# A two-layer graph kernel: the first edge stage sums into a transposed accumulator

## The chip, the cores and the metric

One core of a Trainium2 chip. The metric is the device time of one execution in microseconds (us), the median of three runs. The engines are TensorE (PE; its weight loads PEld), VectorE (DVE), ScalarE (ACT), GpSimd (POOL) and SyncE (SP), with 16 DMA engines beside them. TensorE's clock has two levels, 1.2 and 2.4 GHz; the profile gives the granted clock as a share of the higher one.

## The reference, cut to what matters

6250 nodes with 256 features, 100000 edges sorted by destination, 64 attributes for each edge. First layer:

```
h   = relu(layernorm(x))
e   = relu(edge_attr @ ee_w1 + ee_b1) @ ee_w2 + ee_b2
agg = segment_sum(h[src] + e, dst)      # each node also has an edge to itself, with attributes 0
t   = (1 + eps) * h + agg
t   = relu(ln(t @ w1 + b1)); t = relu(ln(t @ w2 + b2)); y = t @ w3 + b3
x   = x + relu(ln(h + y))
```

The second layer is graph attention over the same edges: scores from both end nodes, a softmax over the edges of a destination, a weighted sum of features, added to x. The change does not touch it.

Since `@ ee_w2` is linear, the kernel sums `relu(edge_attr @ ee_w1 + ee_b1)`, here r, over a node's edges and multiplies the sum by ee_w2 afterwards, once for each node.

## The kernel before, in words

Nodes lie in 50 tiles of 125. An accumulator `acc` [128, 50, 512] in float32 stays in SBUF: for each node (a partition) 256 sums of node features and 256 sums of r. There are five blocks with a barrier after each, and in a block each engine runs its own list of instructions, written out by hand and tied by semaphores.

**Preparation** (`prepare`). Ten chunks c of five tiles. VectorE takes the statistics (`stats`, L264 and L267), ScalarE the root (`deviation`, L216), VectorE the coefficients (L272, L273), ScalarE normalises in place (L222), GpSimd adds ee_b2 into `ht` (L201). ScalarE's `high` (L229) and VectorE's `low` (L284) split `ht` into two float16 halves in `tb`, two slots, which SyncE stores as the gather table `tab0` (L182). VectorE's `own` (L280) writes (2 + eps) times the normalised row plus ee_b2 back into the first half of `acc`. The second half of `acc` starts at zero: half the tiles by GpSimd (L195), half by ScalarE (L232). ScalarE's order is `high(c-2)`, `deviation(c)`, the normalisation of c; VectorE's is `low(c-2)`, `own(c-1)`, `stats(c+1)`, `coefficients(c+1)`. Last on ScalarE is a small DMA of a row of the edge weights (L242), issued after its last `high`, for which it waits; SyncE waits for all stores of the table.

**First edge stage** (`edges0`). 196 batches of 512 edges. GpSimd issues four indirect gathers for each batch (L446) into a ring of six. TensorE computes the edge layer (`edge_mlp`, 8 float16 matmuls of 256 columns, L500 and L501), ScalarE and VectorE split the result into halves (L478, L579). VectorE builds a one-hot matrix edge by node (L325). `sums` then multiplies it with the gathered rows and with r, high and low halves: for each 128 edges the one-hot is the stationary operand and 256 features are the moving one, four matmuls (L507 to L510), 16 for a batch. Where a batch reaches a further tile, `sums` runs once more; it runs 245 times in all. VectorE adds the PSUM tile [125, 512] to the accumulator at a tile index that is read at run time (L556, L569).

**Dense stage** (`nodes`). A software pipeline over tiles: step i does the first layer of tile i, the second layer of tile i-1, the output of tile i-2, and later parts of i-3 and i-4; steps 4 to 47 run in a loop of two. Here features lie on partitions and nodes on the free axis, so the accumulator has to be turned: GpSimd copies tile i+2 of it to `ur` (L813), TensorE's `turn` transposes the r half with two transposes (L868), ScalarE adds the self edge's relu(ee_b1) in `turned` (L1024). `make_h` multiplies by ee_w2 with four float32 matmuls (L918, L922) and turns and adds the own part with two more against the identity (L919), in PSUM. ScalarE's `high_h` (L1070) and VectorE's `low_h` (L1200) split h into halves; `low_h` releases the first layer (semaphore h_split). A float32 matmul is two records in the trace.

TensorE's order in a step i: wait h_split, `layer1(i)`, in it `variance(1)`; two transposes for the scores (L977); wait a_split[0]; `layer2(i-1)`, first half and a quarter of the second, then `variance(0)` for tile i, then the rest; score products; wait a_split[1]; three of eight parts of `output(i-2)`; `make_h(i+1)`; `turn(i+2)`; the rest of the output. layer1 has 48 matmuls, layer2 192, all of 125 columns, the output 24 of 256.

ScalarE's order in a step: `turned`, bias of layer 1 (L1031), deviation(1), bias, squares (L1051), the scores' h2h, `activated(1)` and `high(1)`, deviation(0), bias of layer 2 in two halves (L1031), then `activated(0)`, eight activations (L1059) with `high_h` between the fourth and the fifth, and `high(0)` (L1065). VectorE's `low(0)` (L1189), early in the next step, releases a_split[0]. Late in a step VectorE has scaled(0), row_norm(1), squares (L1165), the score row, `low_h`. GpSimd folds squares (L829 to L831), and clears the accumulator for the second layer (L840) when `make_h` has released it.

The second edge stage and the finish follow; they have the same shape of code before and after.

Of the kernel before, what the change touches and what calls it, by code (L numbers as in the profile page):

```python
# [32 lines left out]
P = 128  # L33
N, D, E, ED, H = 6250, 256, 100000, 64, 1024
TN = 125
# [76 lines left out]
def prepare(nc, t, dram, sb):  # L112


    with ExitStack() as ctx:
        m = Memory(nc, ctx)
        acc, rstd, nmr = sb["acc"], sb["rstd0"], sb["nmr0"]
        CH = NT // PG
# [8 lines left out]
        b2bc = m.sb("p_b2bc", [TN, D], F32)  # L127
        eps1 = m.sb("eps1", [P, 1], F32)
        er = m.sb("er", [P, D], F32)
# [12 lines left out]
        spans_sb = m.sb("spans_sb", [half, 2, 2], I32)  # L142

# [7 lines left out]
        tb_ready, t_free = m.sem("tb_ready"), m.sem("t_free")  # L151
        tb_stored = [m.sem(f"tb_stored{s}") for s in range(2)]
# [35 lines left out]
        def _(pool):  # L188
# [6 lines left out]
            pool.memset(acc[:, 0:NT // 2, D:2 * D], 0.0)  # L195
# [10 lines left out]
        def _(act):  # L206
            act.dma_start(b2bc[:], t["L0_gnn_ee_b2"].partition_broadcast(TN)).then_inc(ld_small, 16)
# [22 lines left out]

            act.wait_ge(consts, 1)
            act.activation(acc[:, NT // 2:NT, D:2 * D], sb["lneps"][:].unsqueeze(2).broadcast_to([P, NT - NT // 2, D]), ACT.Copy, scale=0.0)  # L232
# [10 lines left out]
            act.wait_ge(ewb_done, 16)  # L243

        @block.vector
        def _(dve):
# [29 lines left out]
            def own(c):  # L276

                h = acc[0:TN, tiles(c), 0:D]
                dve.wait_ge(t_ready, c + 1)
                settled(dve.scalar_tensor_tensor(out=h, in0=h, scalar=eps1[0:TN, :], in1=ht[:, c % 2], op0=ALU.mult, op1=ALU.add))  # L280
# [11 lines left out]
            dve.wait_ge(ld_small, 16 * 6)  # L292
            settled(dve.tensor_scalar(eps1[:], eps1[:], 1.0, None, ALU.add))
            settled(dve.tensor_copy(sb["ewa"][:], er[:]))
# [12 lines left out]
            for c in range(CH + 2):  # L307
                if c >= 2:
                    low(c - 2)
                if 1 <= c < CH:  # L310
                    own(c - 1)
# [3 lines left out]
            own(CH - 1)  # L315
# [27 lines left out]
def edges0(nc, t, dram, sb):  # L343


    with ExitStack() as ctx:
# [23 lines left out]
        sum_ps = m.ps("sum_ps", [TN, 3, 2 * D])  # L370
# [120 lines left out]
        def _(pe):  # L491
# [1423 lines left out]
```

## Time and profile before

| | us |
|---|---|
| median of 3 runs | 3159.29 (3156.21 to 3159.81) |
| span of the profiled execution | 3157.3 |
| preparation, to the first instruction of the edge stage | 93.0 |
| first gather issued | 94.1 |
| start of the dense stage | 1107.8 |

Over the whole span TensorE is busy 2446.9 us (77%), VectorE 2156.6 (68%), GpSimd 1976.9 (63%), ScalarE 1488.6 (47%), and the mean granted clock is 0.906. The profiled execution's own time is not listed apart from its span; the span lies 2.0 us under the median of the runs. Busy time is the time in which an engine has an instruction in it; matmuls overlap each other, so neighbouring starts, not durations, tell TensorE's speed. An idle time in brackets names what ended it, "PEq L982" for example the engine's own wait at that line.

### The profile page before, as it was taken

Reading aid. Unit: us, or ns where it says so; the run is one execution under the profiler, and the core shown is the slowest. Engines: PE = TensorE matmul, PEld = TensorE weight load, DVE = VectorE, ACT = ScalarE, POOL = GpSimd, SP = SyncE. Lnnn points to the kernel's source line nnn. Section 1 sums busy time; section 2 is a strip of 40 time slices with the busy share of each in tenths; the row PEclk is TensorE's granted clock in tenths of the full one; section 3 lists DMA queues with packets and bytes.
Section 4 is the critical chain, followed back from the end, with each engine's and each line's share of the span. In section 5 each row is a group of like instructions: output and inputs, shape, how many; then the busy total and the mean of one; then the engine's idle time right before and its main releaser. Section 6 shows DMA issues by size and latency. Waiting matters only on the chain. (4 is left out here: it accounts for less than half of the span.)

```text
span 3157.3 us, 79016 instructions
## 1 busy us (share of the span) xinstructions
PE 2446.9 (77%) x25310; PEld 2164.9 (69%) x25311; DVE 2156.6 (68%) x3833; ACT 1488.6 (47%) x3803; POOL 1976.9 (63%) x2143
## 2 busy tenths in 40 slices
PE   0577777777777789999999999947777777777763
PEld 0466666666666679999999999945555555555552
DVE  7676667777677636666666666657766766666666
ACT  5444444444444458888888888831111111111114
POOL 4677777777777634444444444437777777777772
PEclk9998889999899889999999999978888888887996
DMA  6555555555555500000000000026555655555554
GB/s 158 168 161 149 158 154 166 161 163 160 159 164 158 143 25 18 21 21 20 20 21 20 20 22 21 21 61 178 171 173 173 174 172 168 173 172 173 171 170 136
DMA packets 183839, 373.69 MB, mean 118 GB/s; under 512 B 42598, under 2 KB 93688, under 8 KB 183769
## 3 DMA queue, kind: packets, MB, share of 16 engines
q0 software_dynamic: 75552, 209.66, 23.5%
q1 hardware_dynamic: 107392, 162.37, 17.4%
q10 hardware_dynamic: 824, 0.87, 0.1%
q8 instruction: 27, 0.44, 0.1%
q14 instruction: 44, 0.35, 0.0%
HBM read 346.95 MB, written 25.80 MB: 118 GB/s over the span
## 5 line engine op out<-in xcount | busy, mean ns | idle before, releaser
L446 POOL DMA_INDIRECT rows<-tab_scratch,srcs x784 | 765.7, 977 | 238.7 <-issue 234.1
L1458 POOL DMA_INDIRECT a_rows<-tab_scratch,srcs x784 | 750.5, 957 | 251.7 <-issue 235.8
L1524 PE MATMUL sum_ps<-feat,a_hot 128*125 128x264 f32 x1960 | 601.5, 463 | 237.5 <-DVE feat L1616 121.0
L1524 PEld LDWEIGHTS sum_ps<-feat,a_hot 128*125 128x125 f32 x1960 | 417.4, 222 | 341.7 <-DVE feat L1616 133.9
L876 PE MATMUL z_ps<-ah,w 128*128 128x125 f16 x6400 | 553.8, 219 | 1.0 <-PEq L982 1.0
L876 PE MATMUL z_ps<-al,w 128*128 128x125 f16 x3200 | 542.7, 217 | 0.0
L876 PEld LDWEIGHTS z_ps<-ah,w 128*128 128x128 f16 x6400 | 489.5, 97 | 1.5 <-issue 1.4
L1468 ACT ACTIVATE feat<-d 128x32 f32<-128x32 f32 x196 | 44.9, 229 | 827.0 <-DVE d L1612 566.2
L500 PE MATMUL mlp_ps<-ewa,eab 128*128 128x256 f16 x788 | 203.5, 290 | 284.3 <-PEq L496 283.3
L478 ACT ACTIVATE rh<-mlp_ps 128x1024 f16<-128x1024 f32 x196 | 199.7, 1019 | 358.2 <-ACTq L477 347.7
L829 POOL TENSOR_TENSOR a<-a 128x500 f32<-128x500 f32 x100 | 124.4, 1244 | 372.1 <-POOLq L828 372.1
L507 PE MATMUL sum_ps<-rows,hot 128*125 128x256 f16 x980 | 296.4, 302 | 76.8 <-DMA rows<-tab_scratch,srcs 55.8
L1059 ACT ACTIVATE a<-z,pack 128x125 f32<-128x125 f32 x800 | 321.4, 484 | 11.9 <-ACTq L1055 7.8
L876 PEld LDWEIGHTS z_ps<-al,w 128*128 128x128 f16 x3200 | 315.2, 98 | 0.8
L500 PEld LDWEIGHTS mlp_ps<-ewa,eab 128*128 128x128 f16 x788 | 81.9, 104 | 327.4 <-issue 315.1
L509 PE MATMUL sum_ps<-rh,hot 128*125 128x256 f16 x980 | 291.2, 297 | 0.0
L508 PE MATMUL sum_ps<-rows,hot 128*125 128x256 f16 x980 | 291.1, 297 | 0.0
L510 PE MATMUL sum_ps<-rl,hot 128*125 128x256 f16 x980 | 289.9, 296 | 0.0
L579 DVE SCALAR_TENSOR_TENSOR rl<-mlp_ps,rh 128x1024 f16<-128x1024 f32 x196 | 240.0, 1225 | 34.3 <-DVEq L578 29.2
L1031 ACT ACTIVATE z<-z_ps,pack 128x125 f32<-128x125 f32 x800 | 226.3, 371 | 37.5 <-ACTq L1029 37.5
L1616 DVE TENSOR_TENSOR feat<-a_rows,p_ps 128x1024 f32<-128x1024 f32 x196 | 239.1, 1220 | 3.9 <-DVEq L1404 0.5
L507 PEld LDWEIGHTS sum_ps<-rows,hot 128*125 128x125 f16 x980 | 148.3, 151 | 116.9 <-DMA rows<-tab_scratch,srcs 71.0
(211 smaller groups left out, 5422.8 us busy)
## 6 DMA issues: line engine op xcount, KB each, us to landing
ea<-edge_t SPq DMA_DIRECT2D x394, 128.0 KB
dstb<-dst_flat SPq DMA_DIRECT2D x98, 512.0 KB
rows<-tab_scratch,srcs POOLq DMA_INDIRECT x784
a_rows<-tab_scratch,srcs POOLq DMA_INDIRECT x784
tab_scratch<-prow SPq DMA_DIRECT2D x50, 128.9 KB
hx<-x SPq DMA_DIRECT2D x50, 125.0 KB
x_scratch<-x SPq DMA_DIRECT2D x50, 125.0 KB
hs<-tab_scratch SPq DMA_DIRECT2D x50, 125.0 KB
```

Source lines behind the costliest of these rows:

```text
L446: pool.indirect_dma_start(rows[:, b % DEEP, k, :], None, dram["tab0"], bass.IndirectOffsetOnAxis(ap=srcs[:, c:c + 1], axis=0),).then_inc(r ...
L500: pe.matmul(mlp_ps[:, s, k, :], eab[:, s, e], ewa[:], start=True, stop=False)
L507: pe.matmul(out[:, 0:D], lhs, rows[:, ring, k, 0:D], start=(k == 0), stop=False, skip_group_check=True)
L508: pe.matmul(out[:, 0:D], lhs, rows[:, ring, k, D:2 * D], start=False, stop=False, skip_group_check=True)
L509: pe.matmul(out[:, D:2 * D], lhs, rh[:, s, k, :], start=False, stop=False, skip_group_check=True)
L510: ins = pe.matmul(out[:, D:2 * D], lhs, rl[:, s, k, :], start=False, stop=(k == CB - 1), skip_group_check=True)
L579: dve.scalar_tensor_tensor(out=rl[:, s].rearrange("p k d -> p (k d)"), in0=mlp_ps[:, s].rearrange("p k d -> p (k d)"), scalar=0.0, in1=rh[ ...
L876: ins = pe.matmul(out, lhs, rhs, start=(k == 0 and q == 0), stop=(k == n - 1 and q == 2))
L1059: ins = act.activation(a[j][:, k, :], z[j][:, k, :], ACT.Relu, bias=cols[be][:, k:k + 1], scale=cols[g][:, k:k + 1])
L1458: pool.indirect_dma_start(rows[:, b % DEEP, k, :], None, dram["tab1"], bass.IndirectOffsetOnAxis(ap=srcs[:, c:c + 1], axis=0),).then_inc(r ...
L1524: ins = pe.matmul(out[:], hot[:, h, k, :], feat[:, row, k, :], start=(k == 0), stop=(k == CB - 1))
L1616: return dve.tensor_tensor(feat[:, u, :, 0:D].rearrange("p k (h f) -> p k h f", h=HEADS), slot_of(slot)[:, :, 0:D].rearrange("p k (h f) -> ...
```

## The change

The accumulator of the first layer is kept turned: `accT` is the same memory seen as [128 features, tile, q, 128 nodes], q = 0, 1 for the two halves of the node features and q = 2, 3 for those of r. In `sums` the gathered rows and r become the stationary operand, 128 features wide, and the one-hot the moving one, 125 columns: 32 matmuls for a batch rather than 16. VectorE adds [128, 4, 125]. In the preparation TensorE turns each chunk of the table (20 float16 matmuls against an identity, high and low halves), and ScalarE and VectorE each write one half of the features, scaled and shifted, into `accT`; the self edge's relu(ee_b1) is the start value of the r half. ScalarE's `own(c-3)` stands ahead of `high(c-2)`, and the small DMA of the edge weights' row stands behind the last `own`. In the dense stage GpSimd's copy, `turn`, `turned` and the two own matmuls of `make_h` are gone; `make_h(i+1)` reads `accT` directly and stands behind `variance(0)`, inside the second layer; a new instruction `whole_h` on VectorE adds its PSUM result and the own part into `h32` in SBUF, and `high_h` and `low_h` read that. Variances share a bank and wait for each other's reader (v_read).

```diff
@@ prepare, ScalarE
+            def own(c):
+                act.wait_ge(own_done, c + 1)
+                act.activation(accT[:, tiles(c), 0, 0:TN], own_ps[c % 2][0][:, 0:PG, 0:TN], ACT.Identity,
+                               bias=own_off[:, 0:1], scale=eps2[:]).then_inc(own_kept[0], 1)
...
-            for c in range(CH + 2):
-                if c >= 2:
+            act.wait_ge(own_coef, 1)
+            for c in range(CH + 3):
+                if c >= 3:
+                    own(c - 3)
+                if 2 <= c < CH + 2:
                     high(c - 2)
@@ prepare, TensorE (new)
+            for c in range(CH):
+                pe.wait_ge(tb_ready, c + 1)
+                if c >= 2:
+                    for j in range(KD):
+                        pe.wait_ge(own_kept[j], c - 1)
+                for k in range(PG):
+                    for j in range(KD):
+                        out = own_ps[c % 2][j][:, k, 0:TN]
+                        pe.matmul(out, tb[:, c % 2, k, j * P:(j + 1) * P], ident16[0:TN, 0:TN], start=True, stop=False)
+                        ins = pe.matmul(out, tb[:, c % 2, k, D + j * P:D + (j + 1) * P], ident16[0:TN, 0:TN], start=False, stop=True)
+                ins.then_inc(own_done, 1)
@@ prepare, VectorE
-                dve.wait_ge(t_ready, c + 1)
-                settled(dve.scalar_tensor_tensor(out=h, in0=h, scalar=eps1[0:TN, :], in1=ht[:, c % 2], op0=ALU.mult, op1=ALU.add))
+                dve.wait_ge(own_done, c + 1)
+                dve.tensor_scalar(accT[:, tiles(c), 1, 0:TN], own_ps[c % 2][1][:, 0:PG, 0:TN], eps2[:], own_off[:, 1:2],
+                                  ALU.mult, ALU.add).then_inc(own_kept[1], 1)
@@ edges0, sums
-                    lhs = hot[:, h, k, :]
-                    pe.matmul(out[:, 0:D], lhs, rows[:, ring, k, 0:D], start=(k == 0), stop=False, skip_group_check=True)
...
+                    rhs = hot[:, h, k, :]
+                    for q in range(2 * KD):
...
+                        to = out[:, q, 0:TN]
+                        pe.matmul(to, high, rhs, start=(k == 0 and q == 0), stop=False, skip_group_check=True)
+                        ins = pe.matmul(to, low, rhs, start=False, stop=(k == CB - 1), skip_group_check=True)
@@ nodes, TensorE
-            def make_h(i, p):
...
+            def make_h(i):
                 for j in range(KD):
-                    f = slice(j * P, (j + 1) * P)
-                    pe.matmul(h_ps[:, j, :], w2e[:, 0, f], rt[:, 0, :], start=True, stop=False)
-                    own = pe.matmul(h_ps[:, j, :], ur[:, p, f], ident[0:TN, 0:TN], start=False, stop=False)
...
+                    for k in range(KD):
+                        r = accT[:, bass.ds(i, 1), KD + k, 0:TN].rearrange("p a n -> p (a n)")
+                        ins = pe.matmul(h_ps[:, j, :], w2e[:, k, j * P:(j + 1) * P], r, start=(k == 0), stop=(k == KD - 1))
                 ins.then_inc(h_done, 1)
...
                 if has(i, 0):
                     variance(0)
+                if has(i, 0, 1):
+                    make_h(i + 1)
                 if has(i, 1):
                     layer2(1, range(1, 4), 1 - p)
...
-                    output(range(FIRST))
-                if has(i, 0, 1):
-                    make_h(i + 1, 1 - p)
-                if has(i, 0, 2):
-                    turn(i + 2, p)
-                if has(i, 2):
-                    output(range(FIRST, KH)).then_inc(y_done, 1)
+                    output(range(KH)).then_inc(y_done, 1)
@@ nodes, ScalarE
-                if has(i, 0, 1):
-                    turned(i + 1)
@@ nodes, VectorE
+            def whole_h(i):
+                dve.wait_ge(h_done, 1)
+                dve.sem_inc(h_done, -1)
+                a_own = accT[:, bass.ds(i, 1), 0:KD, 0:TN].rearrange("p a q n -> p (a q) n")
+                dve.tensor_tensor(h32[:], h_ps[:], a_own, ALU.add).then_inc(h_ready, 1)
...
                     row_norm(1, h2[:], x1[:]).then_inc(h2_ready, 1)
+                if has(i, 0, 1):
+                    whole_h(i + 1)
                 if has(i, 1):
                     squares()
```

## Rows read from the trace of the kernel before

**Rows 1.** Stretches (us, busy and instructions of each engine, TensorE's granted clock, DMA share, GB/s).

```profile
93.00:1107.00 1014.00, 743.89 (x5496) 646.62 (x5496) 718.42 (x923) 443.60 (x614) 766.65 (x785) 0.90 0.55 159
1300.00:2000.00 700.00, 700.00 (x10679) 698.61 (x10678) 468.22 (x772) 600.90 (x1619) 307.62 (x407) 1.00 0.07 20
```

**Rows 2.** Groups by shape, first edge stage, 150 to 1100 us (busy, mean ns | idle before, releasers).

```profile
L446 POOL DMA_INDIRECT rows<-tab_scratch,srcs x741 | 723.5, 976 | 225.7 <-issue 221.2 <-DVEq L560 4.6
...
L478 ACT ACTIVATE rh<-mlp_ps 128x1024 f16<-128x1024 f32 x185 | 188.5, 1019 | 344.0 <-ACTq L477 333.4 <-ACTq L475 7.9 <-issue 2.2
...
L507 PEld LDWEIGHTS sum_ps<-rows,hot 128*125 128x125 f16 x928 | 140.4, 151 | 107.5 <-DMA rows<-tab_scratch,srcs 68.4 <-issue 36.9
```

**Rows 3.** Groups by shape, dense stage, 1300 to 2000 us.

```profile
L876 PEld LDWEIGHTS z_ps<-ah,w 128*128 128x128 f16 x4719 | 360.4, 97 | 0.0
```

**Rows 4.** Timeline of a regular dense tile (start us, us, instruction [idle before <-releaser]).

```profile
1601.61 0.28 PE L876 MATMUL gp_ps<-waug,h2h 128*125 128x272 f16 x1
...
1603.29 0.38 PE L918 MATMUL hv_ps<-rt,w2e 128*128 128x125 f32 x2
...
1604.63 0.38 PE L868 MATMUL tv_ps<-ident,ur 125*128 125x125 f32 x2
1604.84 0.27 PE L876 MATMUL y_ps<-w,ah 128*125 128x256 f16 x1
1604.91 0.38 ACT L1070 ACTIVATE hh<-hv_ps 128x250 f16<-128x250 f32 x1 [0.38 <-ACTq L1069]
...
1608.12 1.20 DVE L1189 TENSOR_TENSOR al<-a,ah 128x1000 f16<-128x1000 f32 x1 [0.78 <-DVEq L1188]
...
1609.64 0.22 PE L876 MATMUL z_ps<-ah,w 128*128 128x125 f16 x1
...
1620.65 0.28 PE L876 MATMUL gp_ps<-waug,h2h 128*125 128x272 f16 x1
```

**Rows 5.** The low part of h: duration min/median/max, first and last start.

```profile
L1200 DVE SCALAR_TENSOR_TENSOR hl<-hv_ps,hh x50: 418/419/420, 1115.6 to 2043.4; 128x250 f16<-128x250 f32 x50
```

**Rows 6.** Timeline of tile 1 of the dense stage.

```profile
1134.43 0.21 PE L876 MATMUL z_ps<-ah,w 128*128 128x125 f16 x1 [0.34 <-PEq L982]
...
1145.42 0.44 PE L918 MATMUL hv_ps<-rt,w2e 128*128 128x125 f32 x2
...
1146.98 1.20 DVE L1165 TENSOR_TENSOR a<-z 128x1000 f32<-128x1000 f32 x1 [2.40 <-DVEq L1164]
...
1148.24 0.38 ACT L1070 ACTIVATE hh<-hv_ps 128x250 f16<-128x250 f32 x1
...
1148.76 0.42 DVE L1200 SCALAR_TENSOR_TENSOR hl<-hv_ps,hh 128x250 f16<-128x250 f32 x1 [0.58 <-DVEq L1199]
...
1149.32 0.21 PE L876 MATMUL z_ps<-hh,w 128*128 128x125 f16 x1 [2.13 <-PEq L958]
...
1151.44 1.20 DVE L1189 TENSOR_TENSOR al<-a,ah 128x1000 f16<-128x1000 f32 x1 [2.26 <-DVEq L1188]
```

**Rows 7.** Timeline of the preparation and the start of the edge stage.

```profile
43.93 1.27 ACT L229 ACTIVATE tb<-ht 125x1280 f16<-125x1280 f32 x1 [4.80 <-DMA tab_scratch<-tb]
...
78.26 0.30 ACT L216 ACTIVATE rstd<-mv,lneps 125x5 f32<-125x5 f32 x1 [2.04 <-DVE mv L267]
...
79.01 1.49 DVE L284 TENSOR_TENSOR tb<-ht,tb 125x1280 f16<-125x1280 f32 x1
...
80.84 1.55 DVE L280 SCALAR_TENSOR_TENSOR acc<-acc,eps,ht 125x1280 f32<-125x1280 f32 x1 [0.34 <-DVEq L250]
...
85.25 0.59 ACTq L242 DMA_DIRECT2D ewb<-ebh  x1
86.82 1.49 DVE L284 TENSOR_TENSOR tb<-ht,tb 125x1280 f16<-125x1280 f32 x1 [0.34 <-DVEq L250]
...
93.03 0.69 SPq L406 DMA_DIRECT2D st<-sched_scratch  x1
...
95.85 0.73 DVE L325 SCALAR_TENSOR_TENSOR hot<-dsts,negbase,e_iota_ps 128x500 f16<-128x500 f32 x1 [2.39 <-DMA st<-sched_scratch]
```

More of the change, by code:

```diff
@@ L142, in prepare @@
         spans_sb = m.sb("spans_sb", [half, 2, 2], I32)
+        own_ps = [[m.ps(f"own{s}{j}_ps", [P, 8, P]) for j in range(KD)] for s in range(2)]
         ld_x = [m.sem(f"ld_x{c}") for c in range(CH)]
@@ L151, in prepare @@
         tb_ready, t_free = m.sem("tb_ready"), m.sem("t_free")
+        ld_ecol, own_coef, own_done = m.sem("ld_ecol"), m.sem("own_coef"), m.sem("own_done")
+        own_kept = [m.sem(f"own_kept{j}") for j in range(KD)]
         tb_stored = [m.sem(f"tb_stored{s}") for s in range(2)]
@@ L305, in _ @@
             dve.tensor_copy(spans_sb[:], sched_sb[:].rearrange("p c j -> p j c")).then_inc(sched_ready, 1)
-            for c in range(CH + 2):
-                if c >= 2:
+            for c in range(CH + 3):
+                if 2 <= c < CH + 2:
                     low(c - 2)
-                if 1 <= c < CH:
-                    own(c - 1)
+                if c >= 3:
+                    own(c - 3)
                 if c + 1 < CH:
@@ L314, in _ @@
                     coefficients(c + 1)
-            own(CH - 1)
+            for j in range(KD):
+                dve.wait_ge(own_kept[j], CH)
     return range(m.sems[0].num, m.sems[-1].num + 1)
@@ L732, in nodes @@
         hx_free, h0_ready = sem("hx_free"), sem("h0_ready")
-        v1_read = sem("v1_read")
-        ur_ready, ur_free = sem("ur_ready"), sem("ur_free")
-        t_done, rt_ready = sem("t_done"), sem("rt_ready")
-        h_done, hh_ready, h_split = sem("h_done"), sem("hh_ready"), sem("h_split")
+        v_read = sem("v_read")
+        acc_free = sem("acc_free")
+        h_done, h_ready, hh_ready, h_split = sem("h_done"), sem("h_ready"), sem("hh_ready"), sem("h_split")
         z_done = [sem(f"z{j}_done") for j in (1, 2)]
@@ L862, in _ @@
         def _(pe):
-            def turn(i, p):
-                pe.wait_ge(ur_ready, 1)
-                pe.sem_inc(ur_ready, -1)
-                for k in range(KD):
-                    ins = pe.transpose(t_ps[:, k, :], ur[:, p, D + k * P:D + (k + 1) * P], ident[0:TN, 0:TN])
-                ins.then_inc(t_done, 1)
             def products(out, hi, lo, whi, wlo, n, ks=None, rows=False):
@@ L942, in scores @@
                 ins.then_inc(att_done, 1)
-            turn(0, 0)
             bias_sums()
             pe.wait_ge(ld_w2e, 16)
-            pe.wait_ge(rt_ready, 1)
-            pe.sem_inc(rt_ready, -1)
-            make_h(0, 0)
-            turn(1, 1)
+            make_h(0)
             def body(i, p):
@@ L1017, in _ @@
             act.dma_start(bpack[:, 0:4 * D], t["rows_pack"].partition_broadcast(TN)).then_inc(ld_rows, 16)
-            act.wait_ge(eb_ready, 1)
-            def turned(i):
-                act.wait_ge(t_done, 1)
-                act.sem_inc(t_done, -1)
-                for k in range(KD):
-                    ins = act.activation(rt[:, k, :], t_ps[:, k, :], ACT.Identity, bias=eb1[:, k:k + 1])
-                ins.then_inc(rt_ready, 1)
             def biased(j, b, half):
@@ L1172, in chain_done, with inverse @@
                 dve.sem_inc(chain_sem, -1)
-            def inverse(j, read=None):
+            def inverse(j):
                 dve.wait_ge(sd_ready[j], 1)
                 dve.sem_inc(sd_ready[j], -1)
-                if read is not None:
-                    dve.sem_inc(read, 1)
+                dve.sem_inc(v_read, 1)
                 dve.reciprocal(rstd[j][:], rstd[j][:]).then_inc(rstd_ready, 1)
@@ L1199, in low_h @@
                 dve.sem_inc(hh_ready, -1)
[L1200 removed]
+                dve.scalar_tensor_tensor(out=hl[:], in0=h32[:], scalar=1.0 / WS, in1=hh[:],
                                          op0=ALU.mult, op1=ALU.subtract).then_inc(h_split, 1)
+            def whole_h(i):
[3 more added lines that the diff above has]
+                dve.tensor_tensor(h32[:], h_ps[:], a_own, ALU.add).then_inc(h_ready, 1)
+            whole_h(0)
             low_h()
+            dve.sem_inc(acc_free, 1)
             score_parts()
@@ L1272, in body @@
                     low_h()
+                    dve.sem_inc(acc_free, 1)
                 if has(i, 4):
```

99 lines of the change are left out of this document (51 added, 48 removed).

## The prediction

> **What bounds the kernel now.** I read the stretches first [rows 1]. There are two stages that the change touches for long. In the first edge stage (93 to 1107 us) TensorE is busy for 744 of 1014 us at a mean granted clock of 0.90; in the dense stage (about 1108 to 2108 us, here its regular part) it is busy for 700.00 of 700 us at 1.00. The busy time of a pipelined engine alone is no proof, so the groups come next. In the edge stage GpSimd's gathers take 723.5 us of a stretch of 950, and the idle time before them is 225.7 us, of which 221.2 is its own issue and 4.6 a wait [rows 2]: 949.2 of 950, so GpSimd's gathers set the pace, 5.1 us for each batch of four, and TensorE, VectorE and ScalarE have slack. In the dense stage TensorE streams without a pause, one tile in 19.04 us: (2043.4 - 1148.76) / 47 = 19.03 [rows 5, 6]. But the second limit is close behind, and this is what the whole forecast hangs on.
>
> **The loop behind TensorE.** Call Z the end of a tile's second layer and X the start of the next tile's. TensorE does from Z (1601.61) to X (1609.64) score products, output, make_h with the turns, and the next first layer: 8.03 us [rows 4]. From X to the next Z (1620.65) it needs 11.01 us. Beside this runs a chain: Z, then ScalarE's second half of the bias, four activations, the high part of h, four activations, the high part of the activations, and VectorE's low part of them, which releases X. That low part starts at 1608.12 and takes 1.20, so it ends at 1609.32 [rows 4]; TensorE arrives 0.32 us after that, of which the release takes about 0.15. Slack is under 0.2 us. In that chain ScalarE waits 0.38 us for make_h, until 1604.91 [rows 4]. How long the chain is without that wait is shown by tile 1, where TensorE has no output to compute and make_h comes right behind Z: Z at 1145.42, the high part of h at 1148.24 with no idle before it, the low part at 1151.44 to 1152.64. That is 7.22 us; the same tile's X came at 1134.43 after a wait of 0.34 [rows 6], and X to Z was 10.99. TensorE is released 0.14 us after a VectorE instruction ends (1148.76 + 0.42 to 1149.32) [rows 6]. So the chain Z to X is 7.22 + 0.15 = 7.37 us, and a tile that is bound by it takes 10.99 + 7.37 = 18.36.
>
> **Dense stage, part by part.** Removed from TensorE: two transposes, 1604.84 - 1604.63 = 0.21 us, and two of six float32 matmuls, which take (1604.63 - 1603.29) / 6 = 0.223 each, so 0.45 [rows 4]: 0.66 us a tile, 33 us over 50 tiles if TensorE stayed the bound. But the four matmuls that remain, 0.89 us, are also moved: from between Z and X, where all 1.55 us of make_h and turn stood, to behind variance(0), between X and Z. TensorE's own work from Z to X falls to 8.03 - 1.55 = 6.48 us, less than the chain's 7.37, so the chain decides there. From X to Z it rises to 11.01 + 0.89 = 11.90. New period: 11.90 + 7.37 = 19.27 against 19.04, a loss of 0.23 us a tile. TensorE will wait 0.9 us a tile, in two places: for h_split before the first layer (in tile 1 the low part of h ends at Z + 3.76 [rows 6]; TensorE is ready at Z + 1.68 for the score products and nine output matmuls [rows 4], + 1.64 for fifteen more at 0.11, = 3.32), with the release about 0.6 us, and 0.3 for a_split[0] before the second. Nothing is on the wait's back: behind it in TensorE's queue are just these layers.
> Other edits of the stage: whole_h on VectorE is 250 elements of PSUM and SBUF, priced as the low part of h, 0.42 us [rows 5]. It stands between the row normalisation and the squares, which wait for the bias until Z + 1.56 (1146.98 in tile 1 [rows 6]), so the idle time there hides it; were it not hidden, it would delay the squares of tile i-1, whose variance is wanted 5 us later. ScalarE's two turned activations and GpSimd's copy go; both engines are idle for longer than that and neither piece is in the chain (turned comes after the high part). The wait of v_read is met by the reciprocal issued microseconds before. acc_free stands in front of GpSimd's clearing and its folding, and it is given 3 us before the folding has input. Reading h from SBUF rather than PSUM: from 0 to 0.03 us. Registers for the address of acc on TensorE: hidden by its backlog, up to 0.1 us a tile if not.
> Sum: tiles 1 to 3 lack output or score products and stand nearer to the chain's 18.36; to 19.27 they lose up to 0.9 each, 2.7 us. The other 45 lose 0.23 each, 10.4 us. The start loses a turn, its activations and its hops, at half clock: I take -1.2. The end 0. Together +11.9; bounds: the wait could be 0.1 us a tile shorter or 0.2 longer, +7 to +21.
>
> **First edge stage.** 16 matmuls of 256 columns become 32 of 125 for each batch. Weights were 125 wide and loaded in 151 ns [rows 2]; they become 128 wide, as in the dense stage, where a load takes 97 ns and hides [rows 3]: (11.01 - 0.28) / 192 = 0.056 us for each 125-column matmul at full clock. 32 of them take 1.79 us; 16 of 256 columns at 0.11 (1.68 us for six of 272 and nine of 256 [rows 4]) took 1.76. Cost 0 us of 5.1 us a batch, and TensorE's slack covers more than that. VectorE's add has 500 elements for 512. Value 0, bounds -3 to +6, since the gathers' time (976 ns in the mean [rows 2]) varies with what VectorE does.
> A rule speaks against this part. The Trainium skill (TensorE: Matmul & The Clock Gate, section The mechanism) says that a weight load overlaps running matmuls only if its row group differs. All loads here use all rows, so by it load and stream would take turns. The rows deny it: the 97 ns load fits beside a step of 56 ns. What it would cost is a rival below.
>
> **Preparation.** Each chunk of 5 tiles now also goes through TensorE: 20 matmuls of 125 columns. The engine is otherwise idle here, so I take half clock, 0.11 us each: 2.2 us, and 0.4 for start and drain. VectorE loses 1.55 us [rows 7] and gains an instruction over 625 elements. ScalarE gains 0.7, between 0.38 (250 elements) and 1.02 (1024) [rows 2, 4]. VectorE's own, 625 elements, is taken at 0.8 between its 0.42 for 250 and 1.49 for 1280 [rows 5, 7]. The order matters more: ScalarE's own(c-3) stands ahead of high(c-2), the square root of the next statistics and all that follows. Today ScalarE idles 2.04 us before that square root [rows 7]. From the start of VectorE's split (79.01): 1.49 split, 0.25 semaphores, 2.4 TensorE, 0.15, own 0.7, high 1.2, root 0.3, coefficients 0.4 with their hops: 6.75, against 6.63 now. So 0.1 us a chunk, on six chunks behind the wait of 4.80 us for the stores at 43.93 [rows 7], which swallows what the later start (one more DMA in ScalarE's queue, three small VectorE instructions) costs before it. The end is where it shows: high(9) comes after own(8), which waits for TensorE on the split of chunk 8. That split starts at 79.6 + 6.1 and ends 7.6 later than 79.6; TensorE 2.5, own 0.7, high 1.2, the last split 1.5: it ends at 93.2, not 88.31 [rows 7]. Then own(9) (2.5 + 0.8), and only then the small DMA of the bias row, which was issued at 85.25 before; from issue to use such a DMA took 2.8 us (93.03 to 95.85) [rows 7]. The stage ends at 99.7 instead of 93.03: +6.7, bounds +2 (if the order costs only at the last chunk) to +10.
>
> **Sum** against the profiled execution (span 3157.3 us, which is 2.0 below the median of 3159.3, the runs before spread from 3156.2 to 3159.8): 6.7 + 0 + 11.9 = +18.6, so 3178 us on the scale of the runs. The later stages are not touched.
>
> **Rivals.**
> A, faster: TensorE stays the bound of the dense stage. It needs the chain from Z to X to be shorter than 6.48 us; tile 1 measured 7.22 plus release, and the steady tile 7.71 with a wait of 0.38 and hops. Then the period is 19.04 - 0.66 = 18.38, 50 tiles give -33, with +6.7 for the preparation: 3133 us. For it speaks 700.00 of 700 busy; against it the row of tile 1. Chance 0.13.
> B, as forecast but the preparation is free, since VectorE has 0.7 us less a chunk: 3171 us. Against it the order on ScalarE. Chance 0.10.
> C, load and stream in turn (the rule above): 97 + 56 = 153 ns a matmul, by 32 in 245 groups (196 batches and 49 extra tiles) is 1200 us; the edge MLP's 1568 at 0.11 add 172; 1372 us against the gathers' 784 by 949.2 / 741 = 1004: +368, and 3178 with it is 3546 us. Chance 0.01.
> D, the waits in the dense stage bring the clock down. The edge stage has 0.90 at 73% busy, the dense one 1.00 at 100% [rows 1]. At 0.90 in the dense stage the 11.9 us from X to Z become 13.2: +1.3 by 48, 3240 us. But the waits are 0.9 of 19.3 us, in two pieces. Chance 0.04.
> E, the same mechanism with smaller numbers in both places (a chain 0.15 shorter, the preparation +2): 3164 us. Chance 0.10.
> The forecast itself, 3168 to 3190: 0.62.
>
> **Chances.** A measurement of this kernel tells 0.2% (6.3 us) from no change. Faster: A with some of E's tail, 0.14. Same (3153 to 3165.6): the most of E and a little of B, 0.12. Slower: 0.74. The range, 3158 to 3191, leaves out A, C and D, and about as little of the forecast on either side.
>
> **What would show it.** Right: dense period about 19.27, ScalarE's high part of h without idle before it, TensorE waiting at the h_split and a_split[0] lines, X to Z 11.9; gathers still back to back in the edge stage, its length within 5 us; the first gather at about 101 us instead of 94. Wrong: a period of 18.4 with TensorE full (A), the first gather at 94 (B), TensorE's step over 0.1 us at full clock (C), granted clock under 0.97 in the dense stage (D).

## The result, and the profile after

After the change the kernel takes 3205.24 us in the median (3203.65 to 3206.87, four runs); the kernel before, run beside it on the same chip, takes 3159.55 (3156.21 to 3160.64). The ratio is 1.0144, 95% interval 1.013 to 1.0159: slower by 45.7 us. The forecast was 3178 us with a range of 3158 to 3191: the direction was right, the size was not, and the time lies outside the range.

The two profiled executions (spans 3157.3 and 3204.5) differ by stage as follows. Each stage ends with the first instruction of the next one; "the rest" is the second edge stage and the finish.

| us | before | after | difference | forecast |
|---|---|---|---|---|
| preparation | 93.0 | 105.7 | +12.7 | +6.7 |
| first edge stage | 1014.8 | 1015.9 | +1.1 | 0 |
| dense stage | 1006.1 | 1040.4 | +34.3 | +11.9 |
| the rest | 1043.4 | 1042.6 | -0.8 | 0 |

Stretches of the kernel after, as [rows 1]: the edge stage from its start over the same length, and the regular part of the dense stage.

```profile
106.00:1120.00 1014.00, 748.51 (x9416) 661.73 (x9416) 715.65 (x922) 445.15 (x614) 762.90 (x785) 0.89 0.55 159
1300.00:2000.00 700.00, 659.62 (x10101) 651.01 (x10099) 504.20 (x786) 568.64 (x1498) 276.15 (x355) 1.00 0.07 20
```

The edge stage is as it was, though TensorE issues 9416 instructions for 5496. In the dense stage TensorE now has holes, 40.4 us in 700, at a granted clock that is still 1.00. VectorE is busy 36 us more. The new whole_h explains 36 x 0.41 = 15 of them; the other 21 call for an explanation. The waits of TensorE in the same 700 us put all 40.4 at one line, the wait for h_split (us in total, times, longest):

```profile
PE z_ps L909 <- PEq L982: 40.4, 36, 1.1
```

The groups by shape of the kernel after, edge stage (150 to 1100 us) and dense stage, answer to [rows 2] and [rows 3]:

```profile
L491 POOL DMA_INDIRECT rows<-tab_scratch,srcs x742 | 720.9, 972 | 230.6 <-issue 221.1 <-DVEq L610 9.4
...
L560 PEld LDWEIGHTS sum_ps<-hot,rows 128*128 128x128 f16 x1870 | 198.2, 106 | 2.4
...
L909 PEld LDWEIGHTS z_ps<-ah,w 128*128 128x128 f16 x4531 | 346.4, 97 | 0.0
```

Gathers still stand back to back: 720.9 us in them and 221.1 of their own issue in the 950 us, and 9.4 of waiting. A 128-column weight load takes 106 ns in the edge stage, where the mean granted clock is 0.89, and the stage is no longer for having twice as many of them.

Why the h_split wait is long is in the timelines of one regular tile, VectorE first, then GpSimd, then TensorE, which answer to [rows 4]:

```profile
1618.05 0.43 DVE L1282 SCALAR_TENSOR_TENSOR prow<-gp_ps,bpack 125x272 f32<-125x272 f32 x1
1618.74 1.08 DVE L1202 SCALAR_TENSOR_TENSOR hl<-h,hh 128x250 f16<-128x250 f32 x1 [0.26 <-DVEq L1201]
1619.75 0.64 DVE L1290 COPY st<-prow 125x16 f32 x1
```

```profile
1618.31 1.24 POOL L872 TENSOR_TENSOR a<-a 128x500 f32<-128x500 f32 x1 [4.06 <-POOLq L871]
1619.73 0.63 POOL L873 TENSOR_TENSOR a<-a 128x250 f32<-128x250 f32 x1 [0.18 <-POOLq L866]
```

```profile
1619.97 0.21 PE L909 MATMUL z_ps<-hh,w 128*128 128x125 f16 x1 [1.12 <-PEq L982]
```

The low part of h is 250 elements on 128 partitions, 0.42 us before [rows 5]. Here it takes 1.08: it starts inside GpSimd's fold (1618.31 to 1619.55) and ends 0.27 us after it. TensorE starts the first layer 0.15 us later, after 1.12 us of waiting where 0.6 was forecast. All 50 low parts of h (ns, min/median/max):

```profile
L1202 DVE SCALAR_TENSOR_TENSOR hl<-h,hh x50: 420/1082/1483, 1128.7 to 2090.5; 128x250 f16<-128x250 f32 x50
```

Its operand has moved: h was in PSUM before (`hv_ps`) and is in SBUF now (`h`, in the code `h32`). SBUF as such isn't slow, since the minimum is 0.42. In 48 of the 50 tiles GpSimd's fold had begun before it, and in each of them it ends 0.27 or 0.28 us after the fold. Tile 2 shows the same pair, VectorE and then GpSimd:

```profile
1165.17 1.08 DVE L1202 SCALAR_TENSOR_TENSOR hl<-h,hh 128x250 f16<-128x250 f32 x1 [0.61 <-DVEq L1201]
```

```profile
1164.74 1.24 POOL L872 TENSOR_TENSOR a<-a 128x500 f32<-128x500 f32 x1 [9.37 <-POOLq L871]
```

GpSimd ends at 1165.98, VectorE at 1166.25: again 0.27 later. The two others took 0.42. For tile 0 GpSimd had nothing running (its next instruction began at 1129.88); for tile 1 a copy on GpSimd began 0.21 us after it:

```profile
1128.70 0.42 DVE L1202 SCALAR_TENSOR_TENSOR hl<-h,hh 128x250 f16<-128x250 f32 x1 [0.69 <-DVEq L1201]
...
1145.00 0.42 DVE L1202 SCALAR_TENSOR_TENSOR hl<-h,hh 128x250 f16<-128x250 f32 x1 [1.88 <-DVEq L1201]
1145.21 0.47 POOL L880 COPY acc<-zero 125x264 f32<-125x264 f32 x1 [6.49 <-POOLq L879]
```

An instruction with one tensor input can be held too. The copy `st<-prow` behind the low part of h takes 0.64 us inside GpSimd's second fold (the row of 1619.75 above), and 0.17 in the kernel before, where it starts 0.10 us ahead of that fold (at 1605.87 and 1605.97).

The start of the preparation shows the same thing larger. VectorE and GpSimd of the kernel after:

```profile
15.24 0.15 DVE L332 TENSOR_SCALAR eps<-eps 128x1 f32<-128x1 f32 x1 [6.07 <-DMA eps<-L_gnn_eps]
15.55 7.36 DVE L333 TENSOR_SCALAR own_off<-ecol,eps 128x2 f32<-128x2 f32 x1
...
24.75 1.41 DVE L302 BATCH_NORM_STATS2 stat<-acc 125x6 f32<-125x256 f32 x4 [0.24 <-DVEq L288]
```

```profile
6.32 16.56 POOL L205 TENSOR_SCALAR acc<-ecol 128x3200 f32<-128x3200 f32 x2 [4.04 <-DMA ecol<-cols_pack]
```

An instruction over two elements takes 7.36 us: GpSimd's two new fills (8.28 us each, relu(ee_b1) into its half of `accT`) run until 22.88, and VectorE's instruction ends at 22.91. The first statistics start at 24.75, against 15.46 in the kernel before.

### The profile page after: what moved, and what is told of

Same layout as the page of the kernel before. It is cut to its first block and busy times, and to the rows that moved or that the text cites. A ratio compares the mean times of both kernels' runs of the same rounds, so it can differ in the third digit from the quotient of the medians.

```text
span 3204.5 us, 86737 instructions
## 1 busy us (share of the span) xinstructions
PE 2460.0 (77%) x29130; PEld 2179.0 (68%) x29131; DVE 2212.8 (69%) x3885; ACT 1481.5 (46%) x3714; POOL 1948.8 (61%) x2094
## 5 line engine op out<-in xcount | busy, mean ns | idle before, releaser
L1537 PE MATMUL sum_ps<-feat,a_hot 128*125 128x264 f32 x1960 | 612.6, 470 | 230.4 <-DVE feat L1629 104.7
L1537 PEld LDWEIGHTS sum_ps<-feat,a_hot 128*125 128x125 f32 x1960 | 427.2, 227 | 331.6 <-issue 129.0
L545 PE MATMUL mlp_ps<-ewa,eab 128*128 128x256 f16 x788 | 211.7, 299 | 230.2 <-PEq L541 222.5
L559 PE MATMUL sum_ps<-hot,rows 128*128 128x125 f16 x1960 | 354.4, 234 | 36.5 <-PEq L581 15.7
L559 PE MATMUL sum_ps<-hot,rh 128*128 128x125 f16 x1960 | 353.1, 233 | 0.0
L560 PE MATMUL sum_ps<-hot,rl 128*128 128x125 f16 x1960 | 352.5, 233 | 0.0
L560 PE MATMUL sum_ps<-hot,rows 128*128 128x125 f16 x1960 | 352.3, 233 | 0.0
L1039 ACT ACTIVATE z<-z_ps,pack 128x125 f32<-128x125 f32 x800 | 225.5, 367 | 99.3 <-ACTq L1037 99.3
L559 PEld LDWEIGHTS sum_ps<-hot,rows 128*128 128x128 f16 x1960 | 205.3, 105 | 71.5 <-issue 46.9
```

Source lines behind the costliest of these rows:

```text
L545: pe.matmul(mlp_ps[:, s, k, :], eab[:, s, e], ewa[:], start=True, stop=False)
L559: pe.matmul(to, high, rhs, start=(k == 0 and q == 0), stop=False, skip_group_check=True)
L560: ins = pe.matmul(to, low, rhs, start=False, stop=(k == CB - 1), skip_group_check=True)
L1039: ins = act.activation(z[j][:, k, :], z_ps[j][:, half, (k % 4) * TN:(k % 4 + 1) * TN], ACT.Identity, bias=cols[b][:, k:k + 1], scale=(1.0, ...
L1537: ins = pe.matmul(out[:], hot[:, h, k, :], feat[:, row, k, :], start=(k == 0), stop=(k == CB - 1))
```

## The experiments

All times are medians; ratios are against the kernel before. The profiled executions gave these stages (us; "low h" is the median duration of the low part of h, "period" the time from one regular dense tile to the next).

| kernel | time | ratio (95%) | prep. | edge | dense | period | low h |
|---|---|---|---|---|---|---|---|
| before | 3159.5 | | 93.0 | 1014.8 | 1006.1 | 19.04 | 0.419 |
| after | 3205.2 | 1.0144 (1.013, 1.0159) | 105.7 | 1015.9 | 1040.4 | 19.66 | 1.082 |
| e1 h in PSUM | 3183.9 | 1.0077 (1.006, 1.0094) | 105.4 | 1012.2 | 1020.7 | 19.25 | 0.419 |
| e4 + make_h back | 3175.5 | 1.0054 (1.0037, 1.007) | 105.0 | 1011.3 | 1012.5 | 19.09 | 0.419 |
| e2 fill by VectorE | 3205.9 | 1.015 (1.0133, 1.0167) | 97.9 | 1020.4 | 1040.3 | 19.66 | 1.082 |
| e2b the same, padded | 3197.4 | 1.0123 (1.0106, 1.0141) | 98.4 | 1012.9 | 1040.8 | 19.65 | 1.081 |
| e3 own behind | 3194.6 | 1.0112 (1.0095, 1.0129) | 94.5 | 1015.6 | 1041.2 | 19.66 | 1.082 |
| e5 = e1 + e2b + e3 | 3167.6 | 1.0028 (1.0018, 1.0038) | 89.1 | 1014.1 | 1019.8 | 19.25 | 0.419 |
| e7 = e1 + two ahead | 3146.2 | 0.9962 (0.9947, 0.9976) | 105.2 | 1012.3 | 978.8 | 18.38 | 0.405 |
| e6 = e5 + two ahead | 3125.6 | 0.9893 (0.9875, 0.9912) | 88.8 | 1015.9 | 978.8 | 18.38 | 0.406 |

**e1: h stays in PSUM.** The rivals for the missing 0.39 us of the period are VectorE's operand in SBUF beside GpSimd's fold, and a chain that was sized wrong for another reason (the new whole_h, its wait, the longer X to Z). Only the place of h changes.

```diff
-                dve.tensor_tensor(h32[:], h_ps[:], a_own, ALU.add)
+                dve.tensor_tensor(h_ps[:], h_ps[:], a_own, ALU.add)
-                act.activation(hh[:], h32[:], ACT.Copy, scale=1.0 / WS)
+                act.activation(hh[:], h_ps[:], ACT.Copy, scale=1.0 / WS)
-                dve.scalar_tensor_tensor(out=hl[:], in0=h32[:], ...
+                dve.scalar_tensor_tensor(out=hl[:], in0=h_ps[:], ...
```

> The changed kernel, with h kept in PSUM: whole_h adds the own part onto the PSUM tile in place, and the high and low parts read that tile instead of h32 in SBUF. Theory (port): VectorE's low part of h takes 1.08 us instead of 0.42 because it now has two operands in SBUF and is held up by GpSimd's fold that runs beside it; this delays h_split, the first layer and so the second layer's start by 0.39 us a tile. Then the low part of h goes back to 0.42 us, the dense period falls from 19.66 to about 19.27 (X to Z 11.90, Z to X 7.37), and the time falls by 17 to 20 us, to about 3186. Rival (the order alone): the period of 19.66 comes from where make_h stands; then nothing moves by more than 3 us and the period stays over 19.6.

Measured: 3183.86 us, 21.4 less than after; the dense stage 19.7 less. The low part of h, all 50 of this kernel, and one of them beside the fold that began before it (VectorE, then GpSimd):

```profile
L1201 DVE SCALAR_TENSOR_TENSOR hl<-h_ps,hh x50: 418/419/419, 1124.7 to 2068.0; 128x250 f16<-128x250 f32 x50
```

```profile
1161.88 0.42 DVE L1201 SCALAR_TENSOR_TENSOR hl<-h_ps,hh 128x250 f16<-128x250 f32 x1 [0.58 <-DVEq L1200]
```

```profile
1161.48 1.24 POOL L871 TENSOR_TENSOR a<-a 128x500 f32<-128x500 f32 x1 [9.37 <-POOLq L870]
```

This is the pair of 1165.17 above with 0.40 us between the two starts in place of 0.43, the same fold beside it, and the operand in PSUM: 0.42 for 1.08. So for this instruction neither the fold nor the SBUF operand costs anything alone; the two together do. The period falls to (2068.0 - 1124.7) / 49 = 19.25 in the mean, 19.253 in the regular part; the forecast for the change was 19.27.

**e4: make_h back in its old place,** on top of e1: between the third and the fourth part of the output, with whole_h behind the squares on VectorE (not in the cut below). It asks what it is worth to have moved the 0.89 us of make_h to between X and Z.

```diff
                 if has(i, 0):
                     variance(0)
-                if has(i, 0, 1):
-                    make_h(i + 1)
...
-                    output(range(KH)).then_inc(y_done, 1)
+                    output(range(3))
+                if has(i, 0, 1):
+                    make_h(i + 1)
+                if has(i, 2):
+                    output(range(3, KH)).then_inc(y_done, 1)
```

> As the first of these (h in PSUM), and make_h put back to its old place, between the parts of the output, with whole_h behind the squares. Theory (the chain from Z to X sets the period together with what TensorE does from X to Z): X to Z falls by 0.89 us to 11.0; the high part of h now waits for make_h, about 0.6 us, so Z to X is about 8.0; the period is about 19.0, 0.65 us less than 19.66 and 0.25 less than the first experiment: about 3175 us. Rival (TensorE's sum of work sets the period, wherever make_h stands): the same time as the first experiment.

Measured: 3175.45 us, period 19.09. Counted from the start of the score transposes, the second layer starts (X) at 0.52 and ends (Z) at 11.52, so X to Z is back at 11.00 (11.89 in e1), but Z to X is 8.09, against 7.36: the high part of h starts at Z + 3.54 instead of Z + 2.8, because it must wait for make_h and whole_h, and the chain is longer by that. TensorE still waits 9.4 us in the 700 at h_split. Moving make_h trades 0.89 us between X and Z for 0.73 in the chain; in neither place is the period shorter than the 19.04 of the kernel before.

**e2 and e2b: the fill goes to VectorE,** before it waits for its small loads. The rivals for the preparation's start are that VectorE was held up by GpSimd's fills, and that the added small instructions and the DMA of the load were late by themselves.

```diff
@@ GpSimd
-            for j in range(KD):
-                pool.tensor_scalar(accT[:, 0:NT // 2, KD + j, :], ecol[:, 0, j:j + 1]... , 0.0, None, ALU.max)
+                # e2b only: two instructions over one element keep the list as long
+                pool.tensor_scalar(ptmp[:, j:j + 1], ecol[:, 0, j:j + 1], 0.0, None, ALU.max)
@@ VectorE
+            dve.wait_ge(ld_ecol, 16)
+            for j in range(KD):
+                settled(dve.tensor_scalar(accT[:, 0:NT // 2, KD + j, :], ecol[:, 0, j:j + 1]... , 0.0, None, ALU.max))
             dve.wait_ge(ld_small, 16 * 6)
```

> The changed kernel, with the start value of half of the accumulator written by VectorE, while it waits for its small loads, instead of by GpSimd (two instructions of 3200 elements a partition). Theory (port): GpSimd's two instructions (8.3 us each) hold up a VectorE instruction over two elements for 7.4 us, and all of the preparation starts late. Then the first statistics start at about 17 us instead of 24.8, and the first gather falls from 106.8 to about 101, since some of the gain is lost to the later wait for the stores: 4 to 8 us less in all, about 3199. Rival (the order on ScalarE is all that costs in the preparation): the first gather stays within 2 us of 106.8 and so does the time.

Measured: 3205.9 us, no gain, and yet the preparation is 7.8 us shorter. VectorE's own start in e2:

```profile
9.15 3.94 DVE L328 TENSOR_SCALAR acc<-ecol 128x3200 f32<-128x3200 f32 x2
14.40 0.15 DVE L331 TENSOR_SCALAR eps<-eps 128x1 f32<-128x1 f32 x1 [1.31 <-DMA eps<-L_gnn_eps]
14.71 0.23 DVE L332 TENSOR_SCALAR own_off<-ecol,eps 128x2 f32<-128x2 f32 x1
...
16.90 1.73 DVE L298 BATCH_NORM_STATS2 stat<-acc 125x6 f32<-125x256 f32 x5 [0.24 <-DVEq L284]
```

The two-element instruction takes 0.23 for 7.36, and the fill itself 3.94 for GpSimd's 16.56. Of the 7.8 us the edge stage took back 4.5 (1020.4 for 1015.9), and what follows the dense stage is 1.6 longer in this execution (1044.1 for 1042.6), which was not traced. The gathers of e2 are all a little longer (min/median/max):

```profile
L490 POOL DMA_INDIRECT rows<-tab_scratch,srcs x784: 952/957/1913, 99.0 to 1107.8; - x196
```

After the change they were 940/946/1771. 784 gathers by 0.011 us are 8.6, which the edge stage did not show in full against the kernel after. The theory for e2b was that the longer gather belongs to GpSimd's list of instructions, which is two shorter, and not to the fill.

> As e2_fill_vector, but GpSimd keeps two instructions in the place of the two that went, each over a single element a partition. In e2 the preparation became 7.9 us shorter, as the port theory has it, but the time did not: each of the 784 gathers of the first edge stage took 0.957 us in the median instead of 0.946, which is 8.6 us. Theory (GpSimd's list of instructions): that step of 0.011 us depends on what stands ahead of the gathers in GpSimd's list, not on the fill; with the list as long as before the median is 0.946 again, the first gather at 99, and the time about 3198. Rival (what VectorE's shorter start does to the stage): the median stays at 0.957 and the time at 3205.

Measured: 3197.39 us, 7.9 under after; edge stage 1012.9, and the gathers of e2b:

```profile
L494 POOL DMA_INDIRECT rows<-tab_scratch,srcs x784: 942/946/1972, 99.5 to 1100.9; - x196
```

So the two fillers bring the 946 back. Why was not settled: that it is the length of the list, and not something else that the fillers change, is not shown. An edit that takes instructions out of GpSimd's list should be judged with this in mind.

**e3: ScalarE's own behind the next chunk.** The prediction gave the order of `own(c-3)` before `high(c-2)` 0.1 us a chunk and looked for its cost at the end of the stage. Here it stands behind `normalised(c)`, and the small DMA of the bias row is issued ahead of the last three. The two edits were not tried apart.

```diff
             for c in range(CH + 3):
-                if c >= 3:
-                    own(c - 3)
                 if 2 <= c < CH + 2:
                     high(c - 2)
                 if c < CH:
                     deviation(c)
                     normalised(c)
+                if c == CH:
+                    # wait for eb_split, then the DMA of ewb, moved up from behind the loop
+                if c >= 3:
+                    own(c - 3)
```

> The changed kernel, with ScalarE's own(c-3) placed behind the normalisation of chunk c rather than ahead of high(c-2), and the small DMA of the edge weights' row issued before the last own instead of behind it. Theory (order): TensorE's 2.4 us on a chunk then lie beside ScalarE's other work; the chunk's period falls from 6.68 to about 6.0, the last split comes about 4 us sooner after the last coefficients, and the small DMA is out of the end: first gather at about 97 instead of 106.8, the time 3195 to 3198. Rival (the late start is all that costs): the first gather moves by less than 3 us.

Measured: 3194.63 us, 10.6 under after; the stage ends at 94.5 for 105.7, with the first statistics (24.29) nearly as late as in the kernel after (24.75). The period of a chunk shows between two roots (L228) in ScalarE's timeline, of the kernel after and then of e3:

```profile
59.82 0.29 ACT L228 ACTIVATE rstd<-mv,lneps 125x5 f32<-125x5 f32 x1
...
64.57 0.88 ACT L245 ACTIVATE acc<-own_ps,own_off,eps 128x625 f32<-128x625 f32 x1 [1.33 <-PE own_ps L280]
...
66.50 0.29 ACT L228 ACTIVATE rstd<-mv,lneps 125x5 f32<-125x5 f32 x1
```

```profile
62.11 0.30 ACT L228 ACTIVATE rstd<-mv,lneps 125x5 f32<-125x5 f32 x1 [0.41 <-DVE mv L306]
...
67.86 0.30 ACT L228 ACTIVATE rstd<-mv,lneps 125x5 f32<-125x5 f32 x1 [0.41 <-DVE mv L306]
```

6.68 us after (the forecast had 6.75), with ScalarE waiting 1.33 for TensorE in each; 5.75 in e3, where it waits 0.41 for VectorE's statistics instead. So the order costs 0.9 us in every chunk, and the 6.63 of the kernel before, to which the forecast compared, was itself not a floor.

**e5: the three edits together** (e1, e2b, e3).

> The changed kernel with three of the edits together: h in PSUM, the start value written by VectorE (GpSimd's list kept as long), ScalarE's own behind the normalisation and the small DMA ahead of it. Theory (each cost stands by itself): preparation 87 to 89 us (105.7 in the changed kernel, 94.5 with the order mended alone, 97.9 with the fill mended alone), dense stage 1021 us as in e1, the time about 3167. Rival (the two edits of the preparation take away the same wait): preparation not under 93 us, the time 3172 or more.

Measured: 3167.62 us over ten runs (3164.73 to 3171.22), against 3159.5 over fourteen of the kernel before: still slower by 0.28%. Preparation 89.1, which is 3.9 better than before; dense 1019.8, which is 13.7 worse. With the held instructions gone in both places, what is left of the change is a loss in the dense stage, as the prediction's main argument has it.

**e7 and e6: h two tiles ahead.** If the chain from Z to X is what eats the 0.66 us that TensorE saved, taking h off it must bring rival A's period of 18.38. `make_h(i+2)` runs on TensorE between the output's parts (not in the cut below), `high_h` behind `high(0)`, `low_h` behind `low(0)`, `whole_h` last; `hh` and `hl` get two slots. e7 is e1 with this, e6 is e5 with this.

```diff
-        hh = m.sb("hh", [P, KD, TN], F16)
+        hh = m.sb("hh", [P, 2, KD, TN], F16)
@@ ScalarE
-                    activated(0, "g1", "be1", high_h if has(i, 0, 1) else None)
+                    activated(0, "g1", "be1")
                     high(0, p)
+                if has(i, 0, 2):
+                    high_h(p)
@@ VectorE
                     low(0, 1 - p)
+                if has(i, 1, 2) ...:
+                    low_h(1 - p)
...
+                if has(i, 0, 2):
+                    whole_h(i + 2)
```

> As e1 (h in PSUM), but make_h works two tiles ahead instead of one and stands where it stood before, between the parts of the output; hh and hl have two slots, the high part of h comes behind ScalarE's high(0) and the low part behind VectorE's low(0), so nothing of h is left in the chain from Z to X. Theory (two limits side by side, chain from Z to X and TensorE's own work): the chain falls to about 7.1 us, TensorE's own work from Z to X is 6.48 + 0.89 = 7.37, X to Z 11.0, so TensorE is the bound again with a period of 18.38; dense stage about 975 us (before 1006), the time about 3138. Rival (an engine's sum of work, or another chain, keeps the dense period over 19): the time over 3168.

> e7's dense stage with e5's preparation. Theory: preparation 87 to 89 us, edge stage as before, dense stage about 975 us: 3121 us, 38 less than the kernel before the change, which is the saving that the change could have brought. Rival as for e7 and e5: over 3150.

Measured: e7 3146.21 us (3140.6 to 3147.26, five runs), e6 3125.58 (3123.48 to 3128.84, four runs). The dense stage is 978.8 in both, the period 18.38, and TensorE has no hole in the regular part; e6, 1300 to 2000 us:

```profile
1300.00:2000.00 700.00, 700.00 (x10821) 698.55 (x10819) 514.80 (x841) 600.72 (x1603) 309.80 (x380) 1.00 0.07 21
```

That is 38.1 tiles in the stretch for 36.8 before. e7's profiled execution was its fastest run and lies 5.6 us under its median, so its stages add up to less than its time. e6 beats both kernels: 0.9893 of the time before, interval 0.9875 to 0.9912, some 34 us.

## Why the prediction was right and wrong

**Where the time went.** Of +34.3 us in the dense stage, the 45 regular tiles give 45 x 0.62 = 27.9 and the first four transitions 1.5 + 1.8 + 1.5 + 1.4 = 6.2; the start of the stage gives back 0.7 (7.78 to 7.12 us until the first low part of h); 0.9 is left over at the end, not traced further. Of the 0.62 a tile, e1 shows 0.41 to be the held low part of h and leaves 0.21, the forecast's 0.23. Of +12.7 in the preparation, e2b takes back 7.3 (held VectorE) and e3 11.2 (order on ScalarE and the small DMA); together, in e5, 16.6, so the two overlap by about 2 us, and the stage ends 3.9 sooner than in the kernel before.

**Right: that TensorE's 0.66 us would not pay.** In the regular tiles the argument of the chain held to a hundredth. X to Z is 11.90 in the kernel after, as forecast from 11.01 + 0.89 (below from 1603.46 to 1615.37; the next X is at 1623.13), and 11.89 in e1.

```profile
1603.46 0.22 PE L909 MATMUL z_ps<-ah,w 128*128 128x125 f16 x1
...
1615.37 0.28 PE L909 MATMUL gp_ps<-waug,h2h 128*125 128x272 f16 x1
```

Z to X in e1 is 19.25 - 11.89 = 7.36; the forecast took 7.37 from one early tile [rows 6] in which TensorE happened to have no output to compute. A tile of the prologue that lacks one engine's work is where the second limit can be read off. e7 and e6 show the other side: with h off the chain the period is 18.38, the very number of rival A. Rival A was wrong for this kernel and right for the one beside it. The terms for the start of the stage were too small. In e1, where nothing holds h, the first four transitions cost 2.0 + 2.1 + 0.9 + 1.0 = 5.9 us over the kernel before, where the forecast had 2.7 for tiles 1 to 3, and the start gives back 0.6 for 1.2; why was not traced. So e1's dense stage is 14.6 us longer than before, for the forecast's 11.9.

**Wrong: "Reading h from SBUF rather than PSUM: from 0 to 0.03 us."** This is the step that failed. It was priced by the instruction's own length, which indeed is 0.42 in both places when nothing else runs. The neighbour was left out. Before the change, GpSimd's fold overlaps the low part of h in the regular tiles too (the one at 1567.36 lies in a fold from 1566.47 to 1567.71), for nothing, since h is in PSUM. After the change VectorE reads both inputs from SBUF, and it then stands until GpSimd's fold is over: 0.66 us for the instruction, 0.39 for Z to X (7.76 in place of 7.37), 45 times. Over all, e1 is 21.4 us under the kernel after. The difference of 0.3 between 0.66 and 0.39 came out of TensorE's next wait, that for a_split[0], which the forecast had at 0.3: in e1 the second layer starts 0.51 us behind the two score transposes, in the kernel after 0.22, as these rows of TensorE show (e1, then after).

```profile
1609.48 0.38 PE L996 MATMUL gp_ps<-ident,h 125*128 125x125 f32 x2
1609.99 0.22 PE L908 MATMUL z_ps<-ah,w 128*128 128x125 f16 x1
```

```profile
1622.91 0.38 PE L997 MATMUL gp_ps<-ident,h 125*128 125x125 f32 x2
1623.13 0.22 PE L909 MATMUL z_ps<-ah,w 128*128 128x125 f16 x1
```

The Trainium skill (SBUF — State Buffer, section SBUF: two separate sides) has the rule: a VectorE instruction with two SBUF inputs and a GpSimd instruction that reads SBUF contend for one pair of ports, an exclusive lock, and whichever starts first holds it for its whole instruction. The trace agrees: 1.08 us beside a fold begun earlier with h in SBUF, 0.42 with h in PSUM (e1), 0.42 where GpSimd started second (1145.00). The price was in rows of the kernel before: the fold's 1.24 us. So was the effect. There the same line and shape takes 1.11 us beside the fold and 0.41 where GpSimd is idle (`hx` and `h`), and a cast at the very start takes 6.18, ending 0.08 after GpSimd's clearing, where the kernel after, which has no clearing, does it in 0.23. The lines are of the kernel before, the last of the kernel after:

```profile
L1195 DVE TENSOR_SCALAR hx<-hx,mv,rrow 125x256 f32<-125x256 f32 x37 | 41.1, 1111 | 5.6 <-DVEq L1121 5.6
...
L1195 DVE TENSOR_SCALAR h<-x,mv,rrow 125x256 f32<-125x256 f32 x36 | 14.8, 412 | 5.4 <-DVEq L1121 5.4
```

```profile
1.69 6.18 DVE L255 CAST iota<-icol 128x125 f16<-128x125 int32 x1 [0.81 <-POOL ithr L193]
...
2.33 5.46 POOL L195 MEMSET acc<- 128x6400 f32 x1
```

```profile
1.67 0.23 DVE L293 CAST iota<-icol 128x125 f16<-128x125 int32 x1 [0.81 <-POOL ithr L201]
```

**Wrong: the start of the preparation.** It was held that the 4.80 us wait for the stores "swallows what the later start (one more DMA in ScalarE's queue, three small VectorE instructions) costs". The start was 9.3 us late (24.75 for 15.46), not a fraction of one, because one of the three small instructions stood 7.36 us behind GpSimd's fills. The fills themselves, new work of 16.56 us on an engine that had been done at 7.8 (its one clearing), were not priced at all. With this out of the way the stage ends at 98.4 (e2b), where the forecast said 99.7: the chain of the last chunks (TensorE, own, high, split, own, DMA) was of about the right size. The chunk's 6.75 is near the measured 6.68 in part by luck, since its terms as listed add up to 6.89 (and those of the end to 99.3, not 99.7). It was compared with 6.63 before rather than with the 5.75 that the same work allows (e3).

**Right: edge stage.** Forecast 0, bounds -3 to +6; measured +1.1 (and -3.5 to +1.1 over the kernels whose gathers take 946 ns). The gathers remain the pace, and 32 matmuls with their loads fit in TensorE's slack. Rival C, load and stream in turn by 368 us, is out: in the preparation 20 such matmuls, each with its own load, take 2.1 us, 0.105 each, and the edge stage did not move. Rival D is out: the granted clock of the dense stage is 1.00 with holes of 1.1 us. Rival B (preparation free) is out by the 12.7 us of the preparation, rival E (smaller numbers in both places) since both came out larger.

**The range.** Its top, 3191, was made from bounds of costs that the prediction had listed. Most of the error in both stages comes from one mechanism that no bound covered, and both have the same sign: the time less the forecast is 27 us, and e1 and e2b take back 21.4 and 7.9.

## What to carry to other kernels

When a change gives a VectorE instruction its second SBUF operand, or gives GpSimd an instruction where it had been idle, look at what the other of the two engines runs in that stretch. Price the VectorE instruction as if it had to wait for the neighbour's end, not at its own length. The low part of h with its input in PSUM, even added to in place, paid nothing of this. When an engine is at 100% and a chain of the others comes a few tenths of a microsecond behind it, work taken off that engine is worth nothing until the chain is cut too: read the chain's length where the full engine happens to be short of work, and move what can be prepared a tile earlier out of it.

## What the runs showed of the hardware

- VectorE's low part of h, with two SBUF inputs, started inside a GpSimd instruction on SBUF, ends 0.27 or 0.28 us after GpSimd's end in 48 tiles of 50: 1.08 us for 0.42 in the median. The hold also caught an instruction over two elements with inputs in SBUF for 7.36 us, through two GpSimd fills of 8.28 each.
- A one-element VectorE instruction started inside the same fill at 15.24 and took 0.15; so not every one is held. What distinguishes them was not tried.
- Instructions with one SBUF tensor input (beside scalars) were held as well: `hx` at L1195 of the kernel before 1.11 us for 0.41, a copy of 16 elements 0.64 for 0.17, a cast beside GpSimd's clearing 6.18 for 0.23. The trace lists that cast as starting 0.64 us before the clearing, so who started first does not explain this one; the cause stays open.
- Filling 3200 elements on each partition from a broadcast column took GpSimd 8.28 us and VectorE 1.97.
- The median gather was 957 ns in e2 and 946 in e2b, with GpSimd's list two tiny instructions longer: 0.011 us by 784 is 8.6 over the stage, and the edge stage is 7.5 shorter in e2b. The cause stays open.
- 128-column float16 weights load in 97 ns beside a step of 0.056 us in the dense stage (granted clock 1.00). In the preparation 125-column matmuls step at 0.105 us, each with its own load, nearly twice that; the trace has no record of the granted clock before 121.75 us, so the level there is not shown.
